# Two transformer layers on one NeuronCore: V spread by DMA, K in PSUM, and a new order of TensorE's queue in the merged loop

## The reference

```
w = exp(-exp(time_decay + tanh(xw @ td_w1) @ td_w2))
r, k, v = xr @ Wr.T, xk @ Wk.T, xv @ Wv.T      # 32 heads of 8
g = silu(xg @ Wg.T)
def step(s, (r_t, k_t, v_t, w_t)):             # along the 64 rows
    a = k_t[..., :, None] * v_t[..., None, :]
    out = einsum('bhi,bhij->bhj', r_t, u * a + s)
    return a + w_t[..., :, None] * s, out
x1 = x + (groupnorm(out) * g) @ Wo.T
```

## Time and profile before

| what | value |
|---|---|
| device time, median of 3 runs | 1197.81 us (1195.29 to 1200.35) |
| span of the profiled execution, first to last instruction | 1193.3 us |
| device time of the profiled execution itself | not recorded beside its span |
| TensorE busy | 1126.9 us, 94% |
| VectorE busy | 968.7 us, 81% |
| ScalarE busy | 774.8 us, 65% |
| GpSimd busy | 594.3 us, 50% |
| mean granted TensorE clock | 0.990 of full speed |

### The profile page before, as it was taken

One profiled execution on the slowest core, in us unless ns is written; L12 is line 12 of the kernel. 1 busy time (PEld: TensorE's weight loads), 2 busy tenths in 40 slices (PEclk: granted clock), 3 DMA queues, 4 the chain that ended last, 5 costly groups with the idle time before them and its releaser, 6 DMA issues.

```text
span 1193.3 us, 35515 instructions
## 1 busy us (share of the span) xinstructions
PE 1126.9 (94%) x13568; PEld 955.6 (80%) x13568; DVE 968.7 (81%) x1677; ACT 774.8 (65%) x1750; POOL 594.3 (50%) x520
## 2 busy tenths in 40 slices
PE   5899999999999999999999999999999999888898
PEld 5889898889989877777888788877888787667687
DVE  5987778787777761288999999999999999999964
ACT  5778777778778755556755566556755565557475
POOL 5787887877787840243343433434343434343221
PEclk9999999999999989999999999999999999989999
DMA  9400000011111100000000000000000000000001
GB/s 332 139 4 1 0 0 4 20 47 38 46 40 39 45 2 1 1 2 1 1 1 1 2 1 1 0 0 0 0 0 0 0 1 1 10 10 18 18 36 54
DMA packets 25535, 27.31 MB, mean 23 GB/s; under 512 B 2336, under 2 KB 20064, under 8 KB 25056
## 3 DMA queue, kind: packets, MB, share of 16 engines
q1 hardware_dynamic: 25440, 25.99, 6.6%
HBM read 21.79 MB, written 4.19 MB: 22 GB/s over the span
## 4 chain that ended last, share of the span: by engine, by line
PE 72%; DVE 16%; issue 8%; ACT 2%; POOL 1%; DMA 0%; DVEq 0%; ACTq 0%; POOLq 0%
PE psum L953 10%; PE psum L353 9%; PE psum L962 7%; PE psum L267 5%; PE psum L336 5%; PE psum L368 4%; PE psum L1042 4%; PE psum L297 3%; PE psum L1079 3%; DVE shared L1771 3%; PE psum L280 3%; DVE shared L1765 2%; PE psum L1127 2%; PE psum L310 2%; PE psum L1002 2%
## 5 line engine op out<-in xcount | busy, mean ns | idle before, releaser
L1771 DVE TENSOR_TENSOR_SCAN shared<-late_wT,shared 128x512 f32<-128x512 f32 x128 | 184.5, 1442 | 4.4
L863 POOL TENSOR_TENSOR late_xm<-late_mixed,late_xa 128x512 f32<-128x512 f32 x80 | 96.0, 1207 | 162.3 <-DVE late_mixed L1739 156.0
L232 POOL TENSOR_TENSOR shared<-shared,att_row_max 128x512 f32<-128x512 f32 x128 | 132.7, 1056 | 17.4 <-DVE att_row_max L564 17.4
L353 PE MATMUL psum<-shared 128*128 128x128 f32 x1024 | 126.2, 277 | 0.0
L453 ACT ACTIVATE shared<-shared 128x512 f32<-128x512 f32 x128 | 80.4, 631 | 67.9 <-POOL shared L232 67.8
L962 PE MATMUL psum<-w,late_hT 128*128 128x256 f32 x512 | 122.1, 383 | 1.0 <-ACT late_hT L1352 0.9
L872 POOL TENSOR_TENSOR shared<-shared,late_rT 128x512 f32<-128x512 f32 x32 | 41.1, 1284 | 163.6 <-DVE shared L1771 163.6
L353 PEld LDWEIGHTS psum<-shared 128*128 128x128 f32 x1024 | 120.6, 193 | 0.2 <-ACT shared L462 0.2
L564 DVE TENSOR_REDUCE att_row_max<-shared 128x8 f32<-128x512 f32 x128 | 86.9, 680 | 41.0 <-POOL shared L225 41.0
L953 PE MATMUL psum<-late_glnT,w 128*128 128x256 f32 x512 | 118.4, 384 | 1.8 <-ACT late_glnT L1343 1.8
L1765 DVE TENSOR_TENSOR shared<-psum,shared 128x504 f32<-128x504 f32 x128 | 86.7, 678 | 39.1 <-PE psum L1079 37.8
(11 more groups left out here) (170 smaller groups left out, 2656.7 us busy)
## 6 DMA issues: line engine op xcount, KB each, us to landing
shared<-in_enc SPq DMA_DIRECT2D x64, 128.0 KB, 2.6
out<-x SPq DMA_DIRECT2D x16, 256.0 KB, 2.0
x<-in_x SPq DMA_DIRECT2D x7, 512.0 KB, 9.0
w<-in_w SPq DMA_DIRECT2D x2, 1024.0 KB, 16.9
shared<-in_cross_mask SPq DMA_DIRECT2D x1, 1024.0 KB, 11.6
shared<-in_w_qkv SPq DMA_DIRECT2D x1, 768.0 KB, 4.5
x<-in_x SPq DMA_DIRECT2D x2, 256.0 KB, 3.7
shared<-in_w_kv SPq DMA_DIRECT2D x1, 512.0 KB, 12.6
```

Of the source, the lines that this page charges most:

```text
L232: nc.gpsimd.tensor_tensor(zs, zs, peak.unsqueeze(2).to_broadcast([P, PAIRS, S]), ALU.subtract).then_inc(shifted, 1)
L353: last = nc.tensor.matmul(dst[:, half * P:(half + 1) * P], w[:, kb, c0 + half * P:c0 + (half + 1) * P], src[:, u % 2, kb, 0:P], start=(kb ...
L863: nc.gpsimd.tensor_tensor(xm[:, m % 2, :, :].rearrange("p h (b t) -> p (h b) t", t=S), mixed[:, m % 2, :, :].rearrange("p h (b t) -> p (h ...
L1771: nc.vector.tensor_tensor_scan(states, wT[:, u, half, :, :, :].rearrange("p j b t -> p (j b t)"), states, 0.0, ALU.mult, ALU.add).then_inc ...
```

## The change

V is projected like K, channels on partitions, into `proj`, and copied to SBUF as `vT`. Behind the attention phase SP then runs `spread_values` for each run: four DMAs write `vT` to a DRAM tensor `v_rows`, and when these have landed, four DMAs of 512 KB read it back, each row sent to 8 partitions, into `v_rep`, which now holds V as the spreads used to leave it in PSUM. The spreads and `repeat_values` go. The freed banks 6 and 7 hold K, one for even and one for odd runs; R stays in SBUF as before. The products of V and K (`key_values`) are issued one group ahead of the scan on VectorE. The bonus sums are formed with channels on partitions and all 128 partitions are used (`u_sum` is wider and lies in an old bias row); the bonus is added by VectorE's `add_heads`, from PSUM to `o` in SBUF, before the transposition, and `copy_o` goes. `copy_on` writes back to PSUM and `apply_gate` reads it there. `xm` has three buffers. TensorE's list in a body is written anew, as are the places of `copy_in` and the copy of R on ScalarE (`copy_in` first). The waits of single steps follow from these. The diff, cut to its core, first SP:

```diff
+            def spread_values(r, u):
+                sp.wait_ge(copied, r * 3 + NV)
+                sp.nop(nofuse=True)
+                if later(r):
+                    for q in range(SUMS):
+                        sp.wait_ge(v_loaded[q], 16 * r)
+                        sp.nop(nofuse=True)
+                for jl in range(JQ):
+                    sp.dma_start(core.v_rows[:, :, jl, :].rearrange("q h t -> h q t"),
+                                 vT[jl * RH:(jl + 1) * RH, u, :, :]).then_inc(v_written, 16)
+                sp.wait_ge(v_written, 16 * JQ * r + 16 * JQ)
+                sp.nop(nofuse=True)
+                for q in range(SUMS):
+                    half, jq = q % HALVES, q // HALVES
+                    if later(r):
+                        sp.wait_ge(kv_ready, (r - 1) * GROUPS_R + (q + 1) * PER_SUM)
+                        sp.nop(nofuse=True)
+                    sp.dma_start(v_rep[:, q, :, :].rearrange("p j t -> p (j t)"),
+                                 core.v_rows[jq, half * HPH:(half + 1) * HPH, :, :].rearrange("h j t -> h (j t)")
+                                 .unsqueeze(1).to_broadcast([HPH, RS, JQ * RT])).then_inc(v_loaded[q], 16)
```

On TensorE, in `project`:

```diff
+                elif m == NG:
+                    pe.wait_ge(copied, r * 3 + NR)
+                elif m == NR:
+                    pe.wait_ge(copied, r * 3 + NV)
+                elif later(r - 1):
+                    pe.wait_ge(kv_ready, (r - 1) * GROUPS_R)
+                name = {NV: "WvT", NK: "WkT", NR: "WrT", NG: "WgT"}[m]
+                bank = {NV: proj, NK: k_banks[u], NR: proj, NG: proj}[m]
```

TensorE's list in a body, without the parts for the last three runs:

```diff
+                if there(s - 2):
+                    transpose_on(s - 2)
+                if now:
+                    project(s, u, NG)
...
+                if mlp_run:
+                    mlp_transpose(s + 3)
+                if mixing:
+                    mixer(s + 1)
...
+                if now:
+                    bonus_sums(s)
+                if there(s - 2):
+                    project_out(s - 2)
+                if old:
+                    sum_heads(s - 1, 2)
+                    sum_heads(s - 1, 3)
+                if mlp_run:
+                    up(s + 3, 0)
+                    up(s + 3, 1)
+                if mixing:
+                    mix_pair(s + 1, 0)
...
+                if old:
+                    transpose_o(s - 1)
+                if mlp_run:
+                    up(s + 3, 2)
+                    up(s + 3, 3)
...
+                if mixing:
+                    mix_pair(s + 1, 2)
+                    project(s + 1, 1 - u, NW)
+                if now:
+                    sum_heads(s, 0)
+                    sum_heads(s, 1)
...
+                if mixing:
+                    project(s + 1, 1 - u, NV)
+                    decay(s + 1)
+                if mlp_run:
+                    down(s + 3, 0)
+                if mixing:
+                    mix_last(s + 1)
...
+                if mlp_run:
+                    down(s + 3, 1)
...
+                if mlp_run:
+                    down(s + 3, 2)
+                if mixing:
+                    project(s + 1, 1 - u, NK)
+                if norm:
+                    transpose(s + 2)
...
+                if mlp_run:
+                    down(s + 3, 3)
+                if mixing:
+                    project(s + 1, 1 - u, NR)
```

On ScalarE, at the end of a body (`normalise` is not moved):

```diff
                 if there(s + 2):
                     normalise(s + 2)
                 if not s_is(s, RUNS - 1):
                     nc.scalar.preload_act_table_set("gelu_apprx_tanh_and_others")
...
+                if there(s + 2):
+                    copy_in(s + 2)
                 if there(s + 1):
                     copy(s + 1, 1 - u, NR)
...
                 if there(s - 1) and not s_is(s, RUNS - 1):
                     copy_on(s - 1)
-                if there(s + 2):
-                    copy_in(s + 2)
```

On VectorE:

```diff
+                nc.vector.tensor_tensor(
+                    st[:, n, :, :, 1:S],
+                    v_rep[:, n // PER_SUM, n % PER_SUM * JG:(n % PER_SUM + 1) * JG, :].rearrange(
+                        "p j (b t) -> p j b t", t=S)[:, :, :, 0:S - 1],
+                    k_banks[u][:, half * RT:(half + 1) * RT].rearrange("p (b t) -> p b t", t=S)[:, :, 0:S - 1]
+                    .unsqueeze(1).to_broadcast([P, JG, RB, S - 1]),
+                    ALU.mult).then_inc(kv_ready, 1)
...
+            def add_heads(r, u):
+                dve.wait_ge(summed, (r + 1) * SUMS)
+                dve.wait_ge(bonus_v_ready, r + 1)
+                if later(r):
+                    dve.wait_ge(oT_ready, r)
+                nc.vector.tensor_tensor(o[:, :], o_bank, bonus_v[:, u, :], ALU.add).then_inc(o_copied, 1)
...
-                nc.vector.scalar_tensor_tensor(out=yT[:, :], in0=onT[:, :], scalar=0.5, in1=gates[:, u, :], op0=ALU.mult,
+                nc.vector.scalar_tensor_tensor(out=yT[:, :], in0=even, scalar=0.5, in1=gates[:, u, :], op0=ALU.mult,
...
                 for n in range(GROUPS_R):
                     if there(s):
+                        if n + 1 < GROUPS_R:
+                            key_values(s, u, n + 1)
                         scan(s, u, n)
```

More of the change, by code:

```diff
@@ L682 @@
 EARLY = 6
+XM = 3
 def group(n):
@@ L1029, in project @@
                     pe.wait_ge(decay_tanh, r + 1)
[L1030 to L1039, removed]
+                elif m == NG:
[6 more added lines that the diff above has]
+                bank = {NV: proj, NK: k_banks[u], NR: proj, NG: proj}[m]
                 for half in range(HALVES):
                     for kb in range(HALVES):
-                        last = nc.tensor.matmul(proj[:, half * RT:(half + 1) * RT], w[name][:, kb, half * P:(half + 1) * P],
-                                                xm[:, m % 2, kb, :], start=(kb == 0), stop=(kb == HALVES - 1))
+                        last = nc.tensor.matmul(bank[:, half * RT:(half + 1) * RT], w[name][:, kb, half * P:(half + 1) * P],
+                                                xm[m % XM][:, kb, :], start=(kb == 0), stop=(kb == HALVES - 1))
                 last.then_inc(proj_ready, 1)
@@ L1060, in bonus_sums @@
                 if later(r - 1):
-                    pe.wait_ge(onT_copied, r - 1)
+                    pe.wait_ge(y_ready, r - 1)
                 else:
                     pe.wait_ge(mixed_ready, (r + 1) * NMIX)
[L1064 to L1067, removed]
+                for half in range(HALVES):
+                    last = nc.tensor.matmul(even[:, 0:RT], u_sum[:, half, :], bonus[:, half, :],
+                                            start=(half == 0), stop=(half == HALVES - 1))
                 last.then_inc(bonus_sum_ready, 1)
[L1070 to L1081, removed]
             def sum_heads(r, q):
@@ L1552, in body @@
                     ch_normalise(1, 1)
-                if there(s) and not early(s):
-                    repeat_values(s, u, 2)
-                    repeat_values(s, u, 3)
                 if there(s + 3):
@@ L1561, in body @@
                     ch_copy_in(early_run(s, 0), 0)
-                if there(s - 1):
-                    copy_o(s - 1)
-                    if there(s):
-                        set_states(s, 2)
-                        set_states(s, 3)
-                if early(s):
-                    repeat_values(s, u, 2)
-                    repeat_values(s, u, 3)
+                if there(s - 1) and there(s):
+                    set_states(s, 2)
+                    set_states(s, 3)
                 if there(s + 4):
@@ L1919, in body @@
                         gate(s, u)
+                    if n == 2 and there(s - 1):
+                        add_heads(s - 1, 1 - u)
                     if n == 2:
@@ L1965, in _ @@
             ch_finish(EARLY - 1, 1)
+            add_heads(RUNS - 1, 1)
             make_stats(RUNS - 3)
```

213 lines of the change are left out of this document (71 added, 142 removed).

## The result

The changed kernel takes 1270.97 us (median of 4 runs, 1270.38 to 1272.22) where the kernel before took 1198.79: a ratio of 1.0617, 95% interval 1.0593 to 1.064. The profiled execution spans 1268.7 us, 75.4 more than before. The forecast had the sign and the place of the stall, with 1228 us and a range of 1186 to 1248: too low, and outside the range.

What follows compares the result with a forecast made beforehand. The order of TensorE's queue was taken to bound the loop, at 38.45 us a period. The profiled 1193.3 us plus 30.6 gave 1223.9, and 4.5 more for the median made 1228 us, range 1186 to 1248.

Steps and rivals of the forecast that it cites:

- Work taken away: Per period, spreads, repeats and copies removed: TensorE left with 33.5 us of pure work, VectorE with about 34.5.
- V through DRAM hidden: Loop's DMA writes and loads of V, 2.6 to 9.0 us a load, hidden within a period: charged 0.
- The wait behind K: TensorE idle 4.1 us every run before the transposition of xn, waiting for ScalarE's normalise queued behind the copy of K.
- The walk from X to the next X: One loop period followed from the end of xn (X) to the next: 39.95 us at full clock, +1.5 a run.
- The clock: TensorE's gaps of 4.1 and 1.4 to 1.9 us drop it to 1.2 GHz: 1.2 us a run, ends 0 and 3.4.
- the sum: Whole-kernel total of changes, +30.6 us, including +27.0 for ten steady periods at 1.5 + 1.2 each.
- The ends of the loop: Filling pass +4.5 us, the next two runs +1.6, last three runs -2.5, after the loop 0.
- Case 2: Same TensorE stall in the loop but the clock stays at 2.4 GHz: 1213 us, chance 0.23.
- case 1: TensorE stall in the loop with falls of the clock, the main forecast: 1228 us, chance 0.45.
- Case 3: Waits behind K and before the mixer hide, VectorE sets a period of 34.7 us: 1153 us, chance 0.07.
- The half-way case: Wait at L974 but none at the mixer and no clock fall, period 37.8 us: about 1195 us, chance 0.17.
- Case 4: V's loads come too late for a run's first product, over about 9.5 us each: 1280 us, chance 0.08.

Runs made afterwards that it cites:

- e4_both: Changed kernel with head and tail of TensorE's list put back to the old order, new data path kept: 1148.8 us, ratio 0.960.
- e6_no_traffic: e4_both with the DMAs of V left out after run 0, all runs using run 0's V: 1149.2 us, ratio 0.960.
- e1_fill: Changed kernel plus unread identity transpositions on TensorE, 34 between K and the transposition of xn, 12 between G and the MLP transposition: 1228.8 us, ratio 1.026.
- e8_fill_tail: Changed kernel plus only the 34 unread transpositions behind K, the gap before the MLP transposition left empty: 1230.9 us, ratio 1.028.
- e3_head: Changed kernel with bonus sums and output projection put back ahead of MLP transposition and mixer on TensorE: 1239.2 us, ratio 1.035.
- run 0: Not an experiment: a pass of the merged loop of 16 runs of 256 rows, still without output projection and gate product.
- run 2: Not an experiment: a pass of the merged loop of 256 rows; its gate product starts the 11 intervals (424.87 us) measured in the kernel before.
- run 12: Not an experiment: a late pass of the merged loop of 256 rows; its gate product ends the ten steady periods.
- Run -1: Not an experiment: the filling pass of the merged loop.
- run 13: Not an experiment: a late pass of the merged loop of 256 rows, in which output stores are first needed; its gate product ends the 11 intervals.
- run 15: Not an experiment: a pass at the end of the merged loop of 16 runs of 256 rows; its gate product took 0.66 us in the kernel before.
- e7_act_order: Changed kernel, TensorE's list untouched; on ScalarE the next run's log, rstd, normalise and decays ahead of K's copy, except last three bodies: 1175.7 us, ratio 0.983.
- e5_order_old: Kernel before the change with only the transposition of xn moved right behind the K projection, except last three bodies: 1284.2 us, ratio 1.073.
- e2_tail: Changed kernel with the end of TensorE's list (K, down, R, down, transposition of xn) and of ScalarE's put back: 1178.9 us, ratio 0.984.
- e10_fill_half: Changed kernel plus 17 unread transpositions behind K, the gap before the MLP transposition left empty: 1242.9 us, ratio 1.039.

## Why the prediction failed in size

**Work taken away.** Right. It gave TensorE 33.5 us of work and VectorE 34.5 a period; e4_both, which has that work and neither of the two gaps, runs at 34.9 with TensorE busy for 34.0 and VectorE for 33.4. The terms for VectorE add up to 34.0 (35.65 - 0.8 - 0.8), not 34.5.

**V through DRAM hidden.** Right (e6_no_traffic); 6.9 us a load lie between the bounds of 2.6 and 9.0. Four loads at 9.0 with the writes at 2.6 are 38.6 us, not 38.8; nothing hangs on it.

**The wait behind K.** Right: 4.1 us forecast, about 4.0 measured in 13 of 14 runs.

**The walk from X to the next X.** Nearly right: forecast 39.95 us at full clock, 40.6 in e1_fill and in the periods of e8_fill_tail without a fall. G came 4.8 us after X as forecast, the mixer in e8_fill_tail at 672.95 us, 9.15 us after the end of xn near 663.8, against 8.95. The gap ended at the MLP transposition, not at the mixer: that waits for the MLP residual to have read its bank, which I had overlooked, and it changed nothing.

**The clock: the step that failed.** I took 1.2 us a run, "One stretch of 3.4 us at half clock", with 0 and 3.4 (two stretches) as ends. Measured: 8.8 us at 1.2 GHz a run and 3.6 us lost, more than my upper end. What I had wrong is the number of stretches far more than the price of one. One stretch cost 1.6 us (e8_fill_tail), and the gap of 4.0 us by itself brought one in each steady run (e3_head). With the second gap behind it there were two or three a run, and I had taken the two gaps together as the cause of one. The upper end was too low as well: it allowed two stretches, while the trace of the kernel before has a fall of 6.8 us in the loop and one of over 10 ahead of run 0:
```profile
433.10:436.50 3.40, 3.40 (x77) 2.64 (x76) 2.07 (x6) 0.83 (x2) 3.40 (x4) 0.50 0.02 5
436.50:443.30 6.80, 6.12 (x28) 4.80 (x27) 0.36 (x1) 5.03 (x10) 0.65 (x1) 0.50 0.00 0
...
1064.50:1067.90 3.40, 2.71 (x11) 1.66 (x11) 3.40 (x8) 1.23 (x2) 2.61 (x3) 0.51 0.02 5
1067.90:1071.30 3.40, 3.40 (x30) 1.58 (x26) 3.33 (x4) 0.28 (x1) 2.84 (x2) 0.50 0.00 0
```
Why the same short gap is followed by a fall in one run and not in the next stays open: no run varies that alone.

Over the ten periods from the gate of run 2 to that of run 12, the loss is 1038.15 - 598.11 = 440.0 us against 975.22 - 591.19 = 384.0: 56 us where 27 stood in the sum. At 0.65 us the walk makes 6.5 of the missing 29, the clock the rest.

**The ends of the loop.** Run -1 to the gate of run 2: +6.9 us, forecast 4.5 + 1.6. From run 12 to run 13 +4.8 where I had left it at nothing, because VectorE has channel work there: its slack was not enough to cover the stall. From run 13 to 15, -2.5 was forecast, and the gates went from 82.7 to 89.8 us apart, +7.1: there, too, TensorE waits 5.0 us for xn once, and the clock is 0.89 to 0.92 (before 0.96 and 0.92). Behind the loop +0.6. The parts add up to 75.4, against 30.6 in the sum: of the 44.8 us missing, 29 lie in the ten periods and 14.4 between run 12 and run 15. The 4.5 us from the profiled span to the median were 2.3 here.

**The rivals.** Case 2, the clock staying up, is what e1_fill makes of the kernel: 1228.8 us against 1213, for the longer walk and the last runs. That 1228.8 is also the number forecast for case 1 is chance. Case 3 is what both orders together would have given, and is what a sum of removed work alone would forecast: 1148.8 against 1153, with a period of 34.9 against 34.7. The half-way case, a wait at L974 and none at the mixer, has its waits in e3_head, but with a fall of the clock in each run: 41.0 us a period against 37.8, of which the fall explains 1.6 and the rest is not worked out. Case 4 did not occur.

## What to carry to other kernels

With queues in order, removed work is worth nothing until the order lets it through: when a list is written anew, ask of each consumer what stands ahead of its producer on the producer's queue, and in which order that queue waits. A product's first wait on another engine's queue is better put behind two or three pieces of other work (K, down, R, down, transposition) or fed from a producer placed before the wait (e7_act_order). And a gap of TensorE of 4 to 5 us that recurs is to be priced at its length plus the clock: 1.6 us for each 3.4 us at half clock, one such stretch in each steady run where the gap stood alone (e3_head, most of e5_order_old), two or three (3.6 us) where a gap of 1.5 us followed 7 us later. Short gaps are not free either (e2_tail). Filling the gap with idle transpositions recovers the second part until the order is mended.

## What the hardware showed

- A gap of 4.0 us every 44 us left TensorE at 1.2 GHz for 8.8 us of each run, twice the gap's length, and the second stretch began about 7 us after the first had ended (852.2 and 859.1 us), behind a gap of 1.5 us that alone was followed by no fall in the steady loop of e7_act_order and by one in that of e8_fill_tail. The Trainium skill ("TensorE: Matmul & The Clock Gate", Part 1) has idling lower the clock and activity release it; the trace agrees for the first gap, with 0.50 granted from 845.4 us.
- Gaps of 2.1 us with 1.5 after them lowered it in some runs (e10_fill_half, four stretches up to run 12). Gaps of 1.3 and 0.5 us, 0.6 us of work between them, lowered it in most runs of e2_tail (0.50 from 693.1 to 696.5 us). So neither a gap of 2 us nor one of 1.3 is a safe one.
- A single stretch of 3.4 us at half clock in a run cost 1.6 us (e8_fill_tail, period 42.18 against 40.59 us) and 1.5 (e2_tail, 37.66 against 36.15).
- ScalarE's copy from PSUM back to PSUM took about as long as that to SBUF: 0.99 us for two of 256 columns (L1457) against 1.02 in the kernel before (L1460).
